# Sorting tokens to experts: the last group's position one-hots made after the block one-hots, its products last, GpSimd's other waits ahead of it, and other filler products on TensorE

## The reference, cut to what matters

```python
x = x + tanh(g_xattn[0]) * L0_xattn(layernorm(x), ctx, ctx, Wq, bq, Wk, bk, Wv, bv)   # 64 keys a batch, softmax
x = x + tanh(g_ffn[0])   * L0_ffn(layernorm(x), gate_w, w1, w3, w2)
x = x + tanh(g_xattn[1]) * L1_xattn(layernorm(x), ctx, W, b)
x = x + tanh(g_ffn[1])   * L1_ffn(layernorm(x), w1, w2, h1, h2, w3)                   # 256 -> 1024 -> 1024 -> 1024 -> 256

def L0_ffn(x, gate_w, w1, w3, w2):                       # 16 experts, hidden 128, the top 2 of each token
    scores = softmax(x @ gate_w)
    topk_w, topk_idx = top_k(scores, 2)
    topk_w = topk_w / sum(topk_w)
    comb = zeros((T, 16)).at[token, topk_idx].add(topk_w)
    h = silu(einsum('td,edh->teh', x, w1)) * einsum('td,edh->teh', x, w3)
    return einsum('teh,ehd,te->td', h, w2, comb) + x
```

## Time and profile before

| | us |
|---|---|
| median of 3 runs | 515.83 |
| the runs | 514.92, 515.83, 517.38 |
| the profiled execution, its own time | 515.02 |
| its span in the profile | 513.2 |
| TensorE busy | 494.2 (96%) |
| VectorE busy | 317.0 (62%) |
| ScalarE busy | 202.4 (39%) |
| GpSimd busy | 150.6 (29%) |
| mean granted clock of TensorE | 0.981 |

### The profile page before, as it was taken

The page is one execution under the profiler, slowest core; times in us unless marked ns, Lnnn a source line. Parts: engine busy times, 40 slices in busy tenths (PEclk is TensorE's granted clock), DMA queues, the critical chain, the costliest instruction groups (busy, mean ns, idle before and its releaser), DMA issues.

```text
span 513.2 us, 8100 instructions
## 1 busy us (share of the span) xinstructions
PE 494.2 (96%) x2878; PEld 429.6 (84%) x2878; DVE 317.0 (62%) x844; ACT 202.4 (39%) x410; POOL 150.6 (29%) x157
## 2 busy tenths in 40 slices
PE   8998989999989899999999999999999999999996
PEld 7787788999979678888988888897888888788886
DVE  4789954787666568647356874537677633745433
ACT  4467624777763481212244221126222133621210
POOL 1946637766462941101071110125011101000000
PEclk9789989999999999999999999999999999999999
DMA  8935314999976520320041220005032002022101
GB/s 295 407 99 165 114 63 112 290 316 308 317 250 194 197 73 34 91 61 1 2 138 47 68 73 24 0 2 164 22 102 63 0 1 82 1 82 63 41 3 46
DMA packets 34400, 56.59 MB, mean 110 GB/s; under 512 B 4529, under 2 KB 18353, under 8 KB 34322
## 3 DMA queue, kind: packets, MB, share of 16 engines
q1 hardware_dynamic: 29744, 45.03, 27.1%
q0 software_dynamic: 3792, 10.36, 6.7%
q10 hardware_dynamic: 818, 0.61, 0.4%
HBM read 45.63 MB, written 12.32 MB: 113 GB/s over the span
## 4 chain that ended last, share of the span: by engine, by line
PE 85%; DVE 9%; DMA 3%; SPq 1%; issue 1%; ACT 0%; POOL 0%; DVEq 0%; ACTq 0%
PE bank L1681 23%; PE bank L1682 23%; PE bank L1650 6%; PE bank L1647 6%; PE bank L1316 4%; PE bank L1318 4%; PE bank L1317 4%; PE bank L1323 3%; PE bank L1714 3%; PE bank L1713 3%; PE bank L1532 2%; DMA X<-x 2%; DVE ohr L763 1%; DVE stats L681 1%; PE bank L1535 1%; DVE X L674 1%
## 5 line engine op out<-in xcount | busy, mean ns | idle before, releaser
L1289 ACT ACTIVATE sg<-bank,colv 128x512 f32<-128x512 f32 x64 | 44.1, 690 | 188.5 <-PE bank L1682 188.5
L1681 PE MATMUL bank<-Ah,Wr 128*128 128x512 f32 x256 | 100.2, 391 | 0.0
L1681 PE MATMUL bank<-Bh,Wr 128*128 128x512 f32 x256 | 99.9, 390 | 0.0
L1682 PE MATMUL bank<-Al,Wr 128*128 128x512 f32 x256 | 99.7, 390 | 0.0
L1682 PE MATMUL bank<-Bl,Wr 128*128 128x512 f32 x256 | 99.7, 389 | 0.0
L1681 PEld LDWEIGHTS bank<-Ah,Wr 128*128 128x128 f32 x256 | 48.1, 188 | 11.1 <-DVE Al L1039 0.8
L1681 PEld LDWEIGHTS bank<-Bh,Wr 128*128 128x128 f32 x256 | 48.1, 188 | 9.8
L1682 PEld LDWEIGHTS bank<-Bl,Wr 128*128 128x128 f32 x256 | 48.1, 188 | 9.8
L1682 PEld LDWEIGHTS bank<-Al,Wr 128*128 128x128 f32 x256 | 48.1, 188 | 9.7
L1048 DVE CAST Ah<-sg 128x512 fp32r<-128x512 f32 x32 | 13.6, 426 | 62.9 <-ACT sg L1289 62.9
L1650 PE MATMUL bank<-xTl,Wr 128*128 128x512 f32 x128 | 50.5, 394 | 0.2 <-DVE xTl L1017 0.2
(11 more groups left out here) (222 smaller groups left out, 1005.4 us busy)
## 6 DMA issues: line engine op xcount, KB each, us to landing
Wraw<-panels SPq DMA_DIRECT2D x44, 256.0 KB, 4.4
stage<-panels SPq DMA_DIRECT2D x44, 256.0 KB, 2.6
ES<-experts SPq DMA_DIRECT2D x16, 384.0 KB, 5.8
ys_dram<-yb SPq DMA_DIRECT2D x47, 128.0 KB
ys_dram<-x SPq DMA_DIRECT2D x1, 1920.0 KB, 9.7
X<-x SPq DMA_DIRECT2D x3, 512.0 KB, 7.2
xb_dram<-xb SPq DMA_DIRECT2D x3, 512.0 KB, 3.9
out<-outb SPq DMA_DIRECT2D x3, 512.0 KB, 3.3
```

The source lines that it names most:

```text
L1289: eng.activation(sg[:, (8 * layer + m) % 3, :], bank[m % 4][:, :], ACT.Gelu, scale=colv[:, c + m:c + m + 1]).then_inc(f_act[m], 1)
L1681: mm(bank[m % 4][:, :], Wr[:, base:base + P], h[0][:, k, :], start=k == 0, stop=False)
L1682: ins = mm(bank[m % 4][:, :], Wr[:, base:base + P], h[1][:, k, :], start=False, stop=k == FK - 1 and not general)
```

## The change

It has five parts.

1. VectorE: `row_hot` is cut in two. `row_place` (ranks and `pos`) stays in the loop for every group. `row_hot` (the 8 one-hots) stays for groups 0 to 2, and for the last group it is called after the two `ohb`.
2. TensorE: the 32 products run over tiles 0 to 11 of both experts first (24 products) and over the 4 tiles of the last group then (8), which wait for the last `ohr`.
3. TensorE, filler near them: ahead of the products 14 filler products and 9 products of 512 fp16 columns, where 29 stood. Behind them 10, where 20 stood.
4. TensorE: `load_offsets` no longer waits for `pool_step`; that wait comes after both loads and their fillers, with 4 more fillers behind it. Near the start of the program two more fillers stand behind `columns(1, 1)`, and three ahead of `weights_turned(0)`.
5. GpSimd: the waits for `act_setup` and `act_eh` and the two clears come ahead of the wait for `dma_xb`, and that ahead of the wait for `dve_perm`, which is now the last before the gather.

```diff
--- before.py
+++ after.py
@@ -537,14 +537,14 @@
                 split_low(3)
                 factors2(g)
 
-            eng.wait_ge(dve_perm, 1)
-            for b in range(2):
-                eng.wait_ge(dma_xb[b], 16 * rows_stored[b])
             eng.wait_ge(act_setup, ACT_LATE + 2)
 
             eng.wait_ge(act_eh, E)
             for b in range(NXG - 4):
                 eng.sem_clear(dma_exp[b])
+            for b in range(2):
+                eng.wait_ge(dma_xb[b], 16 * rows_stored[b])
+            eng.wait_ge(dve_perm, 1)
             for i in range(NBLK):
                 if i >= NXG:
                     eng.wait_ge(b_tx, i - NXG + 1)
@@ -744,7 +744,7 @@
                                   ranks_of(g).rearrange("p (t e) -> p t e", t=TG).unsqueeze(1)
                                   .to_broadcast([P, TOPK, TG, E]), ALU.mult).then_inc(dve_rk, 1)
 
-            def row_hot(g):
+            def row_place(g):
 
                 eng.wait_ge(dve_rk, g + 1)
                 own(eng.reduce_sum(rnk[:, g, :, :], rtmp[:, :, :, :], AX.X))
@@ -753,6 +753,9 @@
                 own(eng.tensor_scalar(first[:, :, :], rnk[:, g, :, :], BF_P - (P - 1) / 2, None, ALU.add))
                 own.done()
                 own(eng.scalar_tensor_tensor(pos[:, g, :, :], rnk[:, g, :, :], float(BF_P), first[:, :, :], ALU.add, ALU.subtract))
+                own.done()
+            def row_hot(g):
+
                 own.done()
                 if g == 0:
                     eng.wait_ge(act_rep, 2)
@@ -815,7 +818,9 @@
                 rows_added(g)
                 statistics2(g)
                 rank_picked(g)
-                row_hot(g)
+                row_place(g)
+                if g < NG - 1:
+                    row_hot(g)
 
             eng.wait_ge(pe_rank, NG + 1)
             own(eng.tensor_scalar(cup[:, :], bank[2][:, P:P + E], BF_P + (P - 1) / 2, None, ALU.add))
@@ -844,6 +849,8 @@
 
                 eng.tensor_tensor(ohb[:, r, :, :], kbrep[:, :, :],
                                   pblk16[:, r, :].unsqueeze(1).to_broadcast([P, NBLK, NT]), ALU.is_equal).then_inc(dve_ohb, 1)
+
+            row_hot(NG - 1)
 
             own(eng.tensor_scalar(bexp[:, :], pinc[:, :], 1.0 / P, kc[:, K_TOK:K_TOK + 1], ALU.mult, ALU.is_le))
             own.done()
@@ -1453,6 +1460,7 @@
             ins.then_inc(pe_setup, 1)
             eng.wait_ge(act_setup, ACT_QKB)
             columns(1, 1)
+            keep_clock(bank[2], 2)
             eng.wait_ge(act_setup, ACT_TG)
             eng.wait_ge(act_setup, ACT_VT)
             for b in range(NB):
@@ -1463,6 +1471,7 @@
                     ins = mm(dst[:, D:DE], VT[:, k, b * KEYS:(b + 1) * KEYS], QKx[:, k, 0, KEYS:SC], start=k == 0,
                              stop=k == DK - 1)
                 ins.then_inc(pe_setup, 1)
+            keep_clock(bank[2], 3)
             weights_turned(0)
             scores(1)
             eng.wait_ge(act_setup, ACT_V + NB - 1)
@@ -1498,12 +1507,19 @@
             for t in range(NT):
                 ins = mm(mm_counts, ones16[:, :], both[:, t, :], start=t == 0, stop=t == NT - 1)
             ins.then_inc(pe_rank, 1)
-            keep_clock(bank[5], 29)
-            eng.wait_ge(dve_ohr, NG)
-            for n in range(TOPK * NT):
-                r, t = divmod(n, NT)
+            keep_clock(bank[5], 14)
+
+            eng.wait_ge(act_rep, 3)
+            for _ in range(9):
+                mm(bank[5][:, :], ones16[:, :], kbrep[:, 0:PANEL // NT, :].rearrange("p b t -> p (b t)"), start=True, stop=True)
+            eng.wait_ge(dve_ohr, NG - 1)
+            early = T // P - TG
+            places = [(r, t) for r in range(TOPK) for t in range(early)] + [(r, t) for r in range(TOPK) for t in range(early, NT)]
+            for n, (r, t) in enumerate(places):
                 if t == 0:
                     eng.wait_ge(dve_ohb, r + 1)
+                if t == early:
+                    eng.wait_ge(dve_ohr, NG)
                 ins = mm(bank[2][:, 0:NBLK], ohr[:, t // TG, r * TG + t % TG, :], ohb[:, r, :, t], start=n == 0,
                          stop=n == TOPK * NT - 1)
             ins.then_inc(pe_perm, 1)
@@ -1561,13 +1577,14 @@
             offsets = {}
             eng.wait_ge(pool_el, EL_CUT * POOL_EL)
             eng.wait_ge(act_setup, ACT_LATE + 2)
-            keep_clock(bank[5], 20)
+            keep_clock(bank[5], 10)
             eng.wait_ge(dve_perm, 2)
-
-            eng.wait_ge(pool_step, 3)
             for i in range(0, NBLK, OFFS):
                 load_offsets(i)
                 keep_clock(bank[5], 7)
+
+            eng.wait_ge(pool_step, 3)
+            keep_clock(bank[5], 4)
             turns(0)
             turns(1)
             eng.wait_ge(dve_el, E - POOL_EL)
```

## The result

The changed kernel took 512.94 us, median of 20 runs (509.53 to 517.06). The kernel before took 515.15 beside it, median of 20 (514.03 to 517.89). The ratio is 0.9948 with a 95% interval of 0.9930 to 0.9966. So it is faster, by 2.2 us by the medians and 2.7 by the ratio. The forecast was 508.9 us, a gain of 6.9 on the 515.83 that stood on record, and its range ended at 512.5: the direction was right, the gain was less than half of the forecast, and the median lies 0.4 us above the range. The profiled execution took 511.81 us, with a span of 510.0 and a mean granted clock of 0.987. The executions differ by their clock: of the 20, the ten with a mean granted clock of 0.983 or more have a median of 512.1 us, the ten with 0.980 or less one of 513.2.

The account below looks back on a forecast made before the run. TensorE, busy 96% of the span, was taken as the bound. From 515.02 us, 2.8 (A) and 3.7 (B to D) came off, giving 508.5, stated as 508.9 with half of the runs' 0.8 offset; range 506.5 to 512.5.

Parts of the forecast that it names:

- What bounds the kernel: Whole kernel: TensorE is busy 96% of the span, so only less on its path or a higher clock saves time.
- Part A: Near the start: five fillers in the waits for `VT` and `pr` keep the clock up, saving 2.8 us (bounds 0 and 3.13).
- The rival of a clock that falls in spite of the fillers: Near the start: the clock falls anyway, A is worth 0, the median is 512 us; chance 0.20.
- The argument for A: Near the start, against the clock falling anyway: fillers keep the higher clock wherever they stand in a row, as in 60:62.
- Part B: Last group's permutation: reordering VectorE and TensorE starts `spare` 1.7 us earlier, and `perm` moves with it.
- Part C: Behind the 32 products: fewer fillers and earlier register loads; last product to first turn 8.3 us instead of 10.2.
- Part D: GpSimd before the first gather: waits and clears moved ahead save 0.5 us (between nothing and 0.99), hidden, worth 0.
- The cover of part C: At the first block: the first gather, started about 69.9, lands at 72.6 to 75.7, before the fillers end at 77.1.
- the case of A worth nothing with B and C whole: Start fillers save nothing but the later 3.7 us hold: 511.3 to 511.7 us, as a median 512; chance 0.20.

Follow-up runs that it names:

- the filled gaps: The change plus filler products in TensorE's gaps ahead of `ranks` of groups 1 to 3; ratios to the kernel before 0.9921, 0.9912, 0.9913.
- the experiment with fewer fillers: The change with gaps ahead of `ranks` filled, and fewer fillers from the 32 products to the first block; 511.90 us, ratio 0.9916 to the kernel before.
- late panels: The change with the dense layers' weight panels loaded from block 7 on instead of block 4; 525.46 us, ratio 0.9926 to the kernel before.

## Why the prediction was wrong, and what of it held

**What bounds the kernel** was read rightly. What was won up to the first block came from three things: the low clock near the start, the order of VectorE's queue, and the fillers on the path.

**Part A, forecast 2.8 us: right in the profiled execution (2.62 at `pos`), wrong as a sum.** This is the step that failed. It took a low level seen in one execution for a fixed cost, and asked what the fillers would save there. It did not ask where TensorE would stand idle once it was done sooner. The scores came early, TensorE was ahead of VectorE, and the wait for `both` in group 1 grew from 1.05 to 2.0 us. Behind a gap of 1.94 to 2.01 us there the clock fell in six of seven profiles, which cost 1.7 or 3.0 us of the 2.6. By itself A gave 1.0004 [0.9978, 1.0029], and with the gaps filled 0.9978. The rival of a clock that falls in spite of the fillers had a chance of 0.20 and the right price, 512 against 512.94 measured; it came true, at 38 us rather than at 19. That its number fits so well is in part luck: in the first profile the clock fell at neither place, and the loss lay behind the first block. That the gap is the cause rests on the filled gaps: seven profiles without a fall at 38, with at most 0.23 us of it left, and 23.4 or 23.5 us every time. The gap does not decide alone: one profile had 2.00 us and no fall. The fillers near the start are no guarantee at 19 either. In two profiles the clock fell there all the same, behind a wait for `VT` of 1.49 us (low for 3.4) and 2.83 us (low for 13.7), and in three others it did not, behind 1.55, 1.71 and 1.71 us. The argument for A, that fillers keep the higher clock wherever they stand in a row, was too wide: the fillers behind the 32 products ran at 0.56 in the prediction's own.

At 38 the drop follows the longest gap up to there (1.94 to 2.01 us), and is gone where the gap is filled. At 66 to 71 no such gap stands ahead of it: in the first profile TensorE is busy without a break from 63.20, with products of 47 columns and then fillers, and the clock is 0.50 from 67.0 to 70.5. The gap of 1.23 us ahead of 63.20 is not needed, since with 14 wide products in it the clock falls there too (66.6).

**Part B, forecast 1.7: 1.72.** `pos` to `perm` is 8.45 or 8.46 us in every profile with the old order and 6.72 to 6.74 in every one with the new. The order of VectorE's queue is fixed work: in each order these times lie within 0.02 us of each other, with 0 to 13.7 us of low level ahead of them.

**Part C, forecast 2.0 beyond B: right in the first profile, 1.5 as a rule.** With 3.4 us of low level behind the products `perm` to the first turn is 7.35 or 7.75 us, against 9.72: 1.97 saved in the first profile. With 6.8 us it is 8.4 to 8.9, with none 7.10. Over the twelve profiles with the new order and the change's own fillers the mean is 8.2, so 1.5 is the usual gain. The nine wide products ahead of the 32 took 2.10 us together, 0.23 each, under the 0.36 that the prediction allowed. The low level was taken to last as before (3.4 us); in seven of the twelve it was twice as long. From the last product to the first turn it took 8.1 us, where 8.3 was forecast. The register loads ran ahead beside the fillers, as assumed; the row of `eoff` after:
```profile
L1534 PEldq TENSOR_LOAD <-eoff x2: 1594/1960/2327, 66.9 to 69.3; - x2
```
**Part D, forecast 0.5 and hidden: 0.07 and hidden.** `perm` to the gather is 1.13 us against 1.20. Moving the waits and clears took 0.07 us off, so they are not what fills the 0.99 us taken as the bound; what does, no run here separates.

**The cover of part C was thinner than said.** The forecast looked only at the first gather, which was there in time. A later one was waited for, 0.7 us, in the first profile. In the experiment with fewer fillers `perm` to the first turn is 1.5 us shorter and the blocks 1.8 us longer, 1.3 of it in waits for gathers.

**The end of the blocks** was not in the forecast, which took the blocks as shifted whole. In the first profile 2.0 us went there, to a wait for stores of `ys` and a low level twice as long. In the execution with filled gaps and a span of 506.1 nothing went there. The experiment with fillers there did not reach the fall, and late panels gave no clear gain. It is not a fixed price of an earlier first block: in another profile of the change the stretch behind the first turn was 432.8 us, against 432.6 before and 435.7 in the first. Its first block turned at 79.06, 1.5 us sooner than before, and its span is 1.3 us shorter (511.9). So the two profiles of the change beside the faster kernel before lost their gain in different places, one behind the first block and one at 38. What makes the end longer in some executions stays open.

**What the missing gain is made of.** 6.5 us were forecast as parts A to C, and 3.1 (0.9940 of 515) were measured over four comparisons. Shown is that A by itself gives nothing, 1.2 us at the most by its interval, and that the fall at 38 costs 1.7 or 3.0 us at `pos` where it comes. Filling the gaps gave 0.8 to 1.4 us back at the end, by the way of counting. Part C's usual 1.5 instead of 2.0 accounts for 0.5. The rest, 1.5 to 2 us, stays open: the blocks, their end and an early fall behind a late `VT` are places where single profiles lost it.

**Range and chances.** Faster had 0.90, and it is faster, by 0.52% in the first comparison and 0.60% pooled. The range missed the median by 0.4 us, since its upper end was the case of A worth nothing with B and C whole, and allowed nothing for a give-back behind the first block.

## What to carry to other kernels

Fillers that saved the clock in one place made TensorE earlier, and its next wait longer (here from 1.05 to 2.00 us): follow TensorE to the next engine it outruns, and fill that too, before a gain is written down. A low clock in one profile is a sample (here 0, 6.8 and 10.2 us of it at one place in executions of one program): look at the granted clock of several executions before it stands as a term, and judge by the distance between two fixed instructions rather than by the end. Work taken out of a fixed chain (here 1.72 us by the order on VectorE) came through at the end of that chain in every profile; whether it reaches the end of the kernel has to be measured apart.

## What was not expected of the hardware

- The clock was low for 10.2 us in a row while TensorE was busy throughout, near 19 in both profiles of the kernel before, near 38 in four others (no pause in the rows of 20:28 and of 40:48, where the clock is 0.50). With the same program it fell for 0, 6.8 or 10.2 us at the same place in different executions.
- Products of 47 columns with no gap between them went with a fall in all but one of the 17 profiles, from 1.1 to 3.8 us behind the first of them on. The fall began 2.2 to 2.8 us behind it with none of the wide products ahead, 1.1 to 3.8 with 9, and 3.5 with 14.
- The same kernel takes 515 us in some comparisons and 530 in others. The first to the last turned block takes 62.1 us in the one and 71.1 in the other at the same number of instructions. The ratios of the change agree all the same (0.9895 and 0.9948 in the faster, 0.9931 and 0.9951 in the slower). The cause was not looked for.
